# Experts' lower product in 16-bit halves, four states to a scan, and gates without the subtraction of their maximum

## What is computed

```python
# branch 1: a state-space scan, 16 states for each channel
xf = depthwise_conv(xn, conv_w, conv_b)
dt = sigmoid(xf @ dt_w.T + dt_b) * (DT_MAX - DT_MIN) + DT_MIN
s  = exp(dt * A) * s + (dt * xf) * b          # over 256 positions, for 16 states
y  = sum over the states of s * c
# branch 2: 16 heads of causal attention, then 8 dense experts (no routing)
out  = softmax(10 * l2norm(q) @ l2norm(k).T, causal) @ v ; out = out @ Wo
h    = layernorm(out, ln_g, ln_b)
gate = softmax(h @ gate_w + gate_b)
hid  = gelu(h @ w1[e] + b1[e])                # 128 -> 512, for each expert e
moe  = sum over e of gate[e] * (hid @ w2[e] + b2[e])   # 512 -> 128, the lower product
return x + y + layernorm(moe, ln_g, ln_b)
```

## Time and profile before

| | us |
|---|---|
| three runs | 1157.93, 1163.9, 1164.41 |
| median | 1163.9 |
| span of the profiled execution | 1155.9 |

### The profile page before, as it was taken

The page is one execution under the profiler, slowest core; times in us unless marked ns, Lnnn a source line. Parts: engine busy times, 40 slices in busy tenths (PEclk is TensorE's granted clock), DMA queues, the critical chain, the costliest instruction groups (busy, mean ns, idle before and its releaser), DMA issues.

```text
span 1155.9 us, 27543 instructions
## 1 busy us (share of the span) xinstructions
PE 1097.5 (95%) x10435; PEld 915.9 (79%) x10435; DVE 980.3 (85%) x2576; ACT 786.9 (68%) x1772; POOL 269.4 (23%) x324
## 2 busy tenths in 40 slices
PE   4885999999999999999999999999999999999997
PEld 1573788888878888887888888788887888888897
DVE  7779789898898989889898988989899898988663
ACT  5582857768486775948667595866758587685553
POOL 2040312314041231404123130412303132130200
PEclk9795999999999999999999999999999999999899
DMA  7001000000000000000000000000000000000000
GB/s 204 6 1 41 6 6 11 1 11 6 6 11 2 15 2 11 6 6 11 1 16 2 6 10 7 11 1 15 2 6 10 6 11 1 11 2 1 11 2 10
DMA packets 18722, 14.60 MB, mean 13 GB/s; under 512 B 2408, under 2 KB 16160, under 8 KB 18592
## 3 DMA queue, kind: packets, MB, share of 16 engines
q1 hardware_dynamic: 17680, 12.76, 3.7%
q10 hardware_dynamic: 912, 0.09, 0.1%
HBM read 10.75 MB, written 2.10 MB: 11 GB/s over the span
## 4 chain that ended last, share of the span: by engine, by line
PE 86%; DVE 6%; issue 3%; POOL 2%; ACT 1%; POOLq 0%; DVEq 0%; ACTq 0%
PE O L539 19%; PE O L444 15%; PE S L427 7%; PE S L460 5%; PE U L523 5%; PE U L521 5%; PE U L522 5%; PE J L369 5%; PE J L332 4%; PE S L391 3%; PE J L333 3%; PE J L334 3%; PE S L387 3%; PE O L451 3%; DVE mxn L1048 1%
## 5 line engine op out<-in xcount | busy, mean ns | idle before, releaser
L743 ACT ACTIVATE hid<-U,b1c 128x256 f32<-128x256 f32 x512 | 200.6, 474 | 176.9 <-PE U L523 176.7
L539 PE MATMUL O<-w2s,hid 128*128 128x128 f32 x2048 | 251.0, 276 | 0.0
L539 PEld LDWEIGHTS O<-w2s,hid 128*128 128x128 f32 x2048 | 238.6, 192 | 2.9
L444 PEld LDWEIGHTS O<-Vx,P 128*128 128x128 f32 x1536 | 188.6, 192 | 35.3 <-issue 11.0
L444 PE MATMUL O<-Vx,P 128*128 128x66 f32 x1536 | 188.8, 273 | 11.5 <-ACT OT L722 9.0
L1150 DVE TENSOR_TENSOR_SCAN st<-aexp,u 128x256 f32<-128x256 f32 x256 | 175.5, 686 | 2.1 <-ACT aexp L728 2.0
L869 POOL TENSOR_TENSOR raw<-raw,nr 128x512 f32<-128x512 f32 x120 | 122.0, 1042 | 135.8 <-DVE nr L1013 135.8
L716 ACT ACTIVATE P<-S 128x768 f32<-128x768 f32 x128 | 103.7, 810 | 52.8 <-PE S L427 51.1
L877 POOL TENSOR_SCALAR_AFFINE_SELECT P<-P 128x512 f32<-128x512 f32 x128 | 90.9, 710 | 191.9 <-ACT P L716 191.9
L523 PE MATMUL U<-h2h,w1l 128*128 128x256 f16 x480 | 131.4, 274 | 0.0
L522 PE MATMUL U<-h2l,w1h 128*128 128x256 f16 x480 | 131.4, 274 | 0.0
(11 more groups left out here) (193 smaller groups left out, 2116.2 us busy)
## 6 DMA issues: line engine op xcount, KB each, us to landing
xin<-in_L_attn_x SPq DMA_DIRECT2D x16, 128.0 KB, 2.2
xres<-in_L_attn_x SPq DMA_DIRECT2D x16, 128.0 KB, 2.1
hid<-in_L_ffn_w SPq DMA_DIRECT2D x2, 1024.0 KB, 6.5
out_dram<-fin SPq DMA_DIRECT2D x16, 128.0 KB, 1.8
raw<-in_L_ffn_Wq SPq DMA_DIRECT2D x1, 512.0 KB, 4.4
raw<-in_L_ffn_Wk SPq DMA_DIRECT2D x1, 512.0 KB, 5.6
raw<-in_L_ffn_Wv SPq DMA_DIRECT2D x1, 512.0 KB, 6.5
wos<-in_L_ffn_Wo SPq DMA_DIRECT2D x1, 512.0 KB, 11.0
```

The lines of the kernel that those rows point to most:

```text
L444: last = mm(dst, P32[:, p % 3, a, c0:c0 + P], Vx[:, kb, 2 * p + a, :], start=(kb == 0), stop=(kb == t))
L539: last = mm(O[e % 2][:, t * P:(t + 1) * P], hid[:, e % 2, m, t * P:(t + 1) * P], w2s[:, e * FC + m, :], start=(m == 0), stop=(m == FC - 1))
L743: fn(hid[:, e % 2, f % FC, :], U[q % 2][:, m * SEQ:(m + 1) * SEQ], ACT.Gelu_apprx_tanh, bias=b1c[:, f:f + 1], scale=1.0 / WS).then_inc(gel ...
```

## The change

There are three parts.

1. **The lower product.** At the start POOL scales w2 by 64 and splits it into f16 halves `w2h` and `w2l` (`split_w2`, three instructions over 4096 elements per partition, and a small memset). For every half of an expert's hidden values (two for each expert, sixteen for each sequence) POOL then makes `hidh`, the f16 rounding of `hid`, and `hidl`, what is left (`hidden_high`, `hidden_low`). `expert_down` becomes three f16 products for each f32 one, high by high, high by low and low by high, and waits for `hid_low`, where it waited for the gelu. For the last sequence, in the tail, `hidden_high` is on DVE. `expert_up` runs one expert further ahead on PE, and ACT's gelus stand ahead of the copies `high` in each m. The factor 64 is taken out in the gates (L1104's instruction gets a second factor) and put onto b2.
2. **The scan.** `u` is copied three times by POOL (`spread_u`, 768 elements), the decay at position 0 is kept at zero, and one `tensor_tensor_scan` of 1024 elements does four states. A sequence has 4 scans in the place of 16; the 16 additions to `y` stay.
3. **The gates.** The maximum is negated and given to the exponential as its bias; the two subtractions (L1096) are gone.

The wait of `g_step` 7 on the convolution, and the counts of the semaphores, follow from these.

The core of the diff:

```diff
             def expert_down(s, e, weighed):
 
-                pe.wait_ge(gelu_done, s * NE * FC + FC * (e + 1))
+                pe.wait_ge(hid_low, s * NE * 2 + 2 * (e + 1))
                 if s == LAST:
                     pe.wait_ge(acc_done, s * NE * T + T * (e - 1))
                 elif e == 0:
@@ -536,8 +542,11 @@
                     pe.wait_ge(acc_done, s * NE * T + T * (e - 1))
                 for t in range(T):
                     for m in range(FC):
-                        last = mm(O[e % 2][:, t * P:(t + 1) * P], hid[:, e % 2, m, t * P:(t + 1) * P],
-                                  w2s[:, e * FC + m, :], start=(m == 0), stop=(m == FC - 1))
+                        dst = O[e % 2][:, t * P:(t + 1) * P]
+                        hi, lo = hidh[:, e % 2, m, t * P:(t + 1) * P], hidl[:, e % 2, m, t * P:(t + 1) * P]
+                        mm(dst, hi, w2h[:, e * FC + m, :], start=(m == 0), stop=False)
+                        mm(dst, hi, w2l[:, e * FC + m, :], start=False, stop=False)
+                        last = mm(dst, lo, w2h[:, e * FC + m, :], start=False, stop=(m == FC - 1))
                 last.then_inc(w2_ready, 1)
...
-                    if old and 1 <= m < NE:
-                        expert_up(i - 1, m)
+                    if old and m + 1 < NE:
+                        expert_up(i - 1, m + 1)
...
             def gate_exps(s):
-                act.wait_ge(o_vec, s * KO + 14)
-                for t in range(T):
-                    fn(ge[:, t, :], gl[:, t, :], ACT.Exp, accum_out=gs[:, t:t + 1]).then_inc(o_act, 1)
...
                     act.wait_ge(c_vec, s * KC + 5)
-                fn(aexp[:, d, :], dt[:, :], ACT.Exp, scale=negA[:, d:d + 1]).then_inc(a_done, 1)
+                if s == 0 and d == 0:
+                    act.wait_ge(w2_split, 4)
+                fn(aexp[:, d, 1:SEQ], dt[:, 1:SEQ], ACT.Exp, scale=negA[:, d:d + 1]).then_inc(a_done, 1)
...
-                    if q % 2 == 0 and e >= 2:
-                        act.wait_ge(w2_ready, s * NE + e - 1)
+                    from_one(act, hid_low, s * NE * 2 + q - 3)
...
+            def split_w2():
+
+                pool.wait_ge(d_w2, 16)
+                nc.gpsimd.tensor_scalar(W232, W232, WS, None, ALU.mult).then_inc(w2_split, 1)
+                pool.wait_ge(w2_split, 1)
+                nc.gpsimd.tensor_copy(w2h[:, :, :].rearrange("p c n -> p (c n)"), W232).then_inc(w2_split, 1)
+                pool.wait_ge(w2_split, 2)
+                nc.gpsimd.tensor_tensor(w2l[:, :, :].rearrange("p c n -> p (c n)"), W232,
+                                        w2h[:, :, :].rearrange("p c n -> p (c n)"), ALU.subtract
+                                        ).then_inc(w2_split, 1)
+                pool.wait_ge(w2_split, 3)
+                nc.gpsimd.memset(aexp[:, :, 0:1], 0.0).then_inc(w2_split, 1)
+
+            def hidden_high(s, q):
+
+                e, r = divmod(q, 2)
+                pool.wait_ge(gelu_done, s * NE * FC + 2 * (q + 1))
+                from_one(pool, w2_ready, s * NE + e - 1)
+                nc.gpsimd.tensor_copy(hidh[:, e % 2, 2 * r:2 * r + 2, :], hid[:, e % 2, 2 * r:2 * r + 2, :]
+                                      ).then_inc(hid_high, 1)
+
+            def hidden_low(s, q):
+                e, r = divmod(q, 2)
+                pool.wait_ge(hid_high, s * NE * 2 + q + 1)
+                nc.gpsimd.tensor_tensor(hidl[:, e % 2, 2 * r:2 * r + 2, :], hid[:, e % 2, 2 * r:2 * r + 2, :],
+                                        hidh[:, e % 2, 2 * r:2 * r + 2, :], ALU.subtract).then_inc(hid_low, 1)
+
+            def spread_u(s):
+
+                pool.wait_ge(c_vec, (s + 1) * KC)
+                nc.gpsimd.tensor_copy(u[:, 1:DG, :], u[:, 0:1, :].broadcast_to([P, DG - 1, SEQ])).then_inc(u_spread, 1)
...
+                        spread_u(i)
...
-                if new:
-                    for n in range(4):
-                        units(i + 1, 1, n)
+                for e in range(NE):
+                    if old:
+                        for q in (2 * e, 2 * e + 1):
+                            hidden_high(i - 1, q)
+                            hidden_low(i - 1, q)
+                    if new and e < 2:
+                        units(i + 1, 1, 2 * e)
+                        units(i + 1, 1, 2 * e + 1)
+                    if not new and e == 1:
+                        root_o(i)
...
             def tail():
                 x_bias(LAST)
-                root_o(LAST)
-                root_e(LAST - 1)
+                for q in range(2 * NE):
+                    hidden_low(LAST, q)
+                    if q == 1:
+                        root_e(LAST - 1)
                 root_e(LAST)
...
-                    V.tensor_reduce(gm[:, :], gl[:, :, :], AX.X, ALU.max).then_inc(o_vec, 1)
-                elif n == 11:
-                    dve.wait_ge(o_vec, at + 12)
-                    for t in range(T):
-                        V.tensor_scalar(gl[:, t, :], gl[:, t, :], gm[:, t:t + 1], None, ALU.subtract
-                                        ).then_inc(o_vec, 1)
+                    V.tensor_reduce(gm[:, :], gl[:, :, :], AX.X, ALU.max, negate=True).then_inc(o_vec, 1)
...
+            def hidden_high(s, q):
+
+                e, r = divmod(q, 2)
+                dve.wait_ge(gelu_done, s * NE * FC + 2 * (q + 1))
+                dve.wait_ge(w2_ready, s * NE + e - 1)
+                V.tensor_copy(hidh[:, e % 2, 2 * r:2 * r + 2, :], hid[:, e % 2, 2 * r:2 * r + 2, :]
+                              ).then_inc(hid_high, 1)
...
+                    V.tensor_tensor(u[:, 0, :], dt[:, :], xf[:, :], ALU.mult).then_inc(c_vec, 1)
+
+            def scan(s, g):
+
+                dve.wait_ge(a_done, s * DS + (g + 1) * DG)
+                if g == 0:
+                    dve.wait_ge(u_spread, s + 1)
+                if s == 0 and g == 0:
+                    dve.wait_ge(w2_split, 4)
+                from_one(dve, y_done, s * DS + (g - 1) * DG)
+                V.tensor_tensor_scan(st[:, g % 2, :, :].rearrange("p d n -> p (d n)"),
+                                     aexp[:, g * DG:(g + 1) * DG, :].rearrange("p d n -> p (d n)"),
+                                     u[:, :, :].rearrange("p d n -> p (d n)"), 0.0, ALU.mult, ALU.add
                                      ).then_inc(scan_done, 1)
...
-            SCAN_AT = {1: 0, 3: 1, 5: 2, 6: 3, 8: 4, 9: 5}
+            O_AT = {1: (5,), 4: (6, 7), 5: (8,), 6: (9, 10), 8: (12, 13)}
+            O_LAST_AT = {2: (0, 1, 2), 3: (5,), 4: (6, 7, 8), 5: (9, 10), 7: (12, 13), 8: (14,), 9: (15,)}
+            SCAN_AT = {2: 0, 5: 1}
+            ADD_AT = {3: (0,), 4: (1,), 5: (2,), 6: (3,), 8: (4,), 9: (5,)}
...
                     if 2 <= m <= NE:
-                        scan(i, m + 7)
                         add_state(i, m + 7)
+                    if m == 3:
+                        scan(i, 3)
```

More of the change, by code:

```diff
@@ L24 @@
 NL = NP
+DG = 4
+NG = DS // DG
 VW = DH + 2
@@ L829, in body @@
                         with_gelu_and_tanh()
+                    if old and 1 <= m < NE:
+                        gelus(i - 1, m)
                     if new and m > 0 and m in TURN_AT:
```

79 lines of the change are left out of this document (43 added, 36 removed).

## The result

| | before | after |
|---|---|---|
| median of four runs, us | 1164.16 | 1289.87 |
| range of the runs, us | 1157.93 to 1164.68 | 1288.67 to 1292.43 |
| span of the profiled execution, us | 1155.9 | 1290.7 |

The changed kernel is slower: ratio 1.112, with a 95% interval of 1.108 to 1.115. The kernel before runs at about 1158 or at about 1164 us (mean granted clock 0.979 and 0.971), and the ratio takes in both. The forecast was 1289 us.

The account below looks back on a forecast made before the run. PE was taken to bound the kernel, with POOL bounding the changed expert stage. 1155.9 + 9 (prologue) + 112 (14 bodies) + 7.6 (body 15) - 1 (tail) = 1283.5; with 5 more, 1289 us, range 1190 to 1350.

Parts of the forecast that it names:

- What decides: Expert stage: POOL's added casts and subtractions make PE's `expert_down` wait; a body gets 8.0 us longer.
- The marks that I had named: POOL 9 tenths of expert stage, 60% or more of span; PE below 90%; `hidl` waits 8-11 us a body; period 76.
- The lower product: PE, expert stage: 24 16-bit matmuls at 60 ns take 1.40 us an expert for 1.79, gaining 0.39 us.
- rival 4: Lower product on PE gets no faster (100 ns weight load or 81 ns a matmul): 1304 us; 25%, beside any other.
- POOL's price: Expert stage: cast 0.60 us, subtraction 1.16, wait between 0.10; one half 1.86, the stage 33.8 us with scalings.
- What DVE takes: Expert stage: DVE's scans, sums into `y` and short instructions take turns with POOL, adding 6.2 us (3.8 to 8.4).
- The prologue: Start: POOL's split of w2 holds up DVE's scalings and norm steps; +9 us, between 0 and 15.
- Body 15 and the tail: Last body: +8 us less 0.4 from POOL's halves and inverse root; tail: -1 us from faster lower products.
- Scans and gates: DVE saves 1.9 us a sequence on scans and 1.7 on gates, but is not the bound: no effect.
- Rival 1: POOL and DVE don't take from each other in the expert stage: a body 1.8 us longer, 1187 us; 15%.
- Rival 2: Faster: one half on POOL, DVE's share included, costs 1.75 us or less; at the low ends 1119 us; 8%.
- Rival 3: Expert stage: DVE falls behind too, its maxima come late and POOL starves; 3 to 4 us more a body, 1338; 17%.

Follow-up runs that it names:

- e1: Changed kernel with POOL's casts and subtractions of the hidden values on 4 elements of each 512, all waits kept: 1159.0 us, period 66.86 us.
- e6: Changed kernel with one more POOL cast per expert, to a spare tile: 1354.7 us, period 79.61 us.
- e2: Changed kernel with DVE's scans and sums into `y` in the expert stage cut to 4 elements, POOL's work unchanged: 1219.3 us, period 69.89 us.
- e11: Kernel before, with sixteen POOL subtractions per body added in bodies 1 to 14 on tiles nobody waits for: 1198.6 us, period 69.99 us.
- e4: Kernel before with only the long scans and new gates, the lower product staying f32: 1163.7 us, ratio 1.000 to 1.005.
- e7: Changed kernel with the high-half casts on ACT and w2's halves made by ACT and DVE: 1238.5 us, ratio 1.063 to 1.073.
- e8: e7 with sixteen short scans again, the gates staying as changed: 1279.7 us, ratio 1.100 to 1.108.

## Why the prediction was right, and where its sum was off

1. **What decides.** POOL's casts and subtractions set the expert stage, and PE waits. Shown by `e1` and `e6`, and by the windows. The marks that I had named: POOL at 36.7 of 38.0 us in the stage and 66% of the span, PE at 84%, the period 75.28 where 76 was said. One mark was off. PE's waits for `hidl` lead PE's own list, with 83.6 us, but that is 5.6 us a body and not 8 to 11, and over all engines POOL's and ACT's waits stand ahead of them. PE's idle time in the stage is 7.3 us, 2.5 of it for DVE's maxima.
2. **The lower product.** 24 matmuls take 1.34 us (they start 56 ns apart), for 1.40 predicted (24 x 60 ns would be 1.44). Four rows of a bf16 mask in the earlier trace rows were the right row to go by, and rival 4 falls. The 81 ns of the Trainium skill's "TensorE: Matmul & The Clock Gate", Back-to-back issue gap, don't hold for this stream; the trace has 56.
3. **POOL's price.** Cast 0.61 us for 0.60, subtraction 1.16 for 1.16, a half 1.79 for 1.86, since part of the gap was counted twice: the next cast starts before the subtraction's row ends.
4. **What DVE takes.** 5.3 us for 6.2 (`e2`: 5.4). Both this and the term before it were a little high: POOL's stage is 37.95 us, for 40.0 summed. A body was priced at +8.0 and is +7.2, so 14 bodies +100.7 for +112. That the body is off by less than the stage comes from its two ends: the next body's first scores start 2.3 us behind the last subtraction, for 1.5 in the sum, behind DVE's last maxima, and the first cast comes 0.3 us later in the body.
5. **The prologue.** The term that was furthest off for its size, and outside its own range. I had priced the scaling of w2 at 3.5 us, from a select of one input (1091 ns for 1024 elements); it took 10.55. Both read and write 32 bits, so that isn't what sets them apart; why the scaling is so much dearer is not shown. POOL was busy 22.7 us there, not 14 to 16, and +9 became +19.3 (a range up to 15 had been given). That DVE's steps would stand behind POOL's had been said; the +9 took it that they partly slip through, and they stood still for the better part of long instructions, 8.70 us for one.
6. **Body 15 and the tail.** Predicted +7.6 and -1, measured +13.35 together, and in `e1`, with the halves' work gone and the waits kept, the same part is 3.5 us shorter than before. So this too is the halves' work. In body 15, after its second lower product, PE waits 4.77 us for the low halves and then goes on at half the clock; POOL had waited 1.25 us for DVE before the inverse root in its row, and one cast beside DVE's work took 2.60 us. Its windows of the changed kernel:

```profile
1228.50:1233.10 4.60, 0.00 (x1) 0.01 (x1) 4.60 (x3) 0.84 (x2) 4.52 (x4) 0.82 0.00 0
1233.10:1238.20 5.10, 5.10 (x37) 4.41 (x38) 1.05 (x4) 1.68 (x4) 4.86 (x6) 0.50 0.01 3
1238.40:1241.40 3.00, 3.00 (x42) 2.86 (x41) 2.69 (x6) 2.12 (x3) 2.84 (x5) 1.00 0.00 0
```

The clock (the number behind POOL) is granted at 0.50 for 5 us after the gap, which is 1.2 GHz of 2.4, and the lower product's matmuls start 107 ns apart there, for 56. The sum had no term for the clock. The attention stage of this body, which `e2` and `e11` ran at half the clock, is not lengthened here: between the last two `orr` lie 37.2 us, for 37.3 before and 50.2 and 50.1 there. All of the +13.35 lies behind it.

7. **Scans and gates.** "Nothing": `e4` gives 0.3%, with a period 0.55 us longer. Right in size, with a small loss at most. Where DVE is the bound, the long scans are worth 2.5 us a body (`e7` against `e8`).
8. **The rivals.** Rival 1, no turns, falls by `e2` and `e11`. Rival 2, faster, falls by the price of a half: 1.79 us and 0.33 of turns, above the 1.75 from which it decides. Rival 3, DVE too, came true in part. POOL has no gap in the stage, so it didn't starve, and `e6` shows that its work still counts nearly in full; but DVE has the later half of the stage's chain, PE's waits for maxima in this stage rose from 11.4 to 40.2 us in all, and with the casts moved away DVE takes over after 2.2 us.

The terms that were too high (-11 for the bodies) and too low (+10 in the prologue, +1.5 in body 0, +6.7 at the end) come to +7. The median lay 1 us below the span of the profiled execution, where 5 above had been added; each run by itself lies 1.7 to 1.8 us above its own span, and the profiled one was the slowest of the four. That is why the total was met within 1 us, and it is luck: without their signs the errors add up to 30 us, 2.3% of the total. That POOL sets the stage and that DVE takes from it was not luck.

## What to carry to other kernels

Before work is given to an idle engine to unload the bound one, add up the stage for that engine and for the one that it takes turns with; here DVE had 2.6 and 5.2 us of room in the two stages, and work that nobody waited for cost 1.9 us of a body of 68. Judge each DVE instruction by where its operands lie: here those from SBUF stretched beside a busy POOL, and the additions from PSUM didn't. Where a long POOL instruction can't be avoided, cut it into pieces: eight pieces took 2.3 us longer together and brought the first mask 6.5 us forward. And compare variants by their periods before their totals: in two of these runs the last body alone was some 13 us longer at half the clock.

## What the runs showed of the hardware

- **DVE beside POOL, by operand.** Durations by source line in the changed kernel, ns as shortest, middle and longest:

```profile
L1225 DVE SCALAR_TENSOR_TENSOR y<-st,bc,y x240: 469/484/1452, 82.7 to 1252.5; 128x256 f32<-128x256 f32 x120
...
L1186 DVE TENSOR_SCALAR cv<-xnT,cols x16: 405/1197/1199, 57.9 to 1160.3; 128x256 f32<-128x256 f32 x16
...
L1172 DVE SCALAR_TENSOR_TENSOR acc<-O,gate,acc x240: 334/343/353, 180.7 to 1255.5; 128x128 f32<-128x128 f32 x120
```

  The sum into `y` (two operands in SBUF) and the product `cv` (one, in SBUF, 32-bit in and out) grow up to threefold beside POOL's instructions (`cv` took 0.40 us in every body of the kernel before), the addition from PSUM not at all in 240. The Trainium skill's "SBUF — State Buffer", SBUF: two separate sides, says that VectorE and GpSimd share a pair of ports as an exclusive lock, taken for the whole instruction by whoever comes first, and that VectorE needs it for two operands from SBUF or in one of its fast modes. By that rule, the trace agrees in the main: the sum into `y` that began at 630.57, beside a subtraction, ends 0.28 us after it, and a step of 0.19 us took 8.70 us beside a 10.55 us instruction. That step ended at 32.54, though, 1.7 us before the instruction's row does.
- **POOL's rates differ by more than the number of inputs.** In the prologue of the changed kernel, at 4096 elements, the f32 scaling took 2.58 ns an element, the subtraction 2.01, and the cast to f16 0.91.
- **A wait can cost twice.** After a gap of 4.77 us in body 15, and after one of 2.59 us in the stage at 633.52, PE ran at a granted clock of 0.50 for 6.8 and 3.4 us; the kernel before is never at half the clock between 117 and 1089 us. Eight transposes took 1.92 us at 635.59 where they take 1.04. After the gap of 1.98 us at 641.40 the clock stayed full.
